# Weighted sums of values in groups of up to three key tiles, in an attention and expert kernel

## What is computed

```
scores = einsum('bhqd,bhkd->bhqk', q, k) * scale        # q, k: 16 content + 32 rotated channels
attn   = softmax(where(causal, scores, -inf))
out    = einsum('bhqk,bhkd->bhqd', attn, v) @ W_o       # v: 16 channels a head
hmid   = gelu(einsum('td,edi->tei', t, W1) + b1)        # 16 experts, 128 hidden channels
eo     = einsum('tei,eio->teo', hmid, W2) + b2          # then the two best experts, weighted
```

## Time and profile before

| what | value |
|---|---|
| median of three runs | 2926.61 us (2926.41 to 2930.67) |
| the profiled execution | 2921.24 us |
| its span | 2919.5 us |
| mean granted TensorE clock | 0.991 |
| TensorE busy | 2809.9 us, 96% |
| VectorE busy | 1863.1 us, 64% |
| ScalarE busy | 1809.6 us, 62% |
| GpSimd busy | 1248.5 us, 43% |

### The profile page before, as it was taken

How to read it: one execution, slowest core, us unless ns; L and a number is a source line. 1 busy time by engine, 2 the same in 40 slices (tenths; PEclk the granted TensorE clock), 3 DMA queues, 4 the chain that set the end, 5 groups by cost and what they waited for, 6 DMA issues and landing times.

```text
span 2919.5 us, 50632 instructions
## 1 busy us (share of the span) xinstructions
PE 2809.9 (96%) x16460; PEld 1236.1 (42%) x16460; DVE 1863.1 (64%) x4636; ACT 1809.6 (62%) x2148; POOL 1248.5 (43%) x1325
## 2 busy tenths in 40 slices
PE   6899999999999999999999999999999999999999
PEld 2344444444444444444444444444444444444433
DVE  4775666756666666666667666675756757667553
ACT  1346675566755677456674576655766566665687
POOL 4312655136451364414654146531465215561254
PEclk8899999999999999999999999999999999999999
DMA  6204443044430444304532055321453124530353
GB/s 146 51 20 99 113 131 78 2 106 120 124 70 4 116 122 109 71 18 118 124 98 64 23 134 127 84 53 43 122 135 88 34 66 120 128 83 25 78 127 94
DMA packets 177551, 253.01 MB, mean 87 GB/s; under 512 B 51085, under 2 KB 83869, under 8 KB 177197
## 3 DMA queue, kind: packets, MB, share of 16 engines
q1 hardware_dynamic: 169936, 246.98, 33.9%
q10 hardware_dynamic: 7360, 2.80, 0.5%
HBM read 159.13 MB, written 12.63 MB: 59 GB/s over the span
## 4 chain that ended last, share of the span: by engine, by line
PE 83%; DVE 7%; issue 4%; POOL 2%; ACT 2%; DMA 1%; SPq 1%; ACTq 0%; POOLq 0%; DVEq 0%
PE ps L1254 17%; PE ps L1296 16%; PE ps L1314 15%; PE ps L1280 9%; PE ps L428 7%; PE ps L477 4%; PE ps L479 2%; PE ps L548 2%; POOL rest L1493 2%; DVE rest L573 1%; PE ps L518 1%; PE ps L529 1%; PE ps L505 1%; PE ps L536 1%; DVE rest L1423 1%
## 5 line engine op out<-in xcount | busy, mean ns | idle before, releaser
L1386 ACT ACTIVATE rest<-ps 128x1024 f32<-128x1024 f32 x1024 | 994.3, 1025 | 340.6 <-PE ps L1296 340.4
L1368 ACT ACTIVATE rest<-ps 128x1024 f32<-128x1024 f32 (+3 forms) x768 | 610.8, 810 | 539.5 <-PE ps L1254 513.7
L1493 POOL TENSOR_TENSOR rest<-rest 128x512 f32<-128x512 f32 x478 | 633.0, 1324 | 560.0 <-DVE rest L1423 549.3
L1423 DVE SCALAR_TENSOR_TENSOR rest<-ps,b2c,wide 128x512 f32<-128x512 f32 x512 | 383.9, 750 | 490.0 <-PE ps L1314 459.2
L1296 PE MATMUL ps<-wide,w1s 98*128 98x512 f32 x2048 | 655.0, 437 | 11.5 <-ACT rest L1386 8.7
L1314 PE MATMUL ps<-rest,w2s 128*32 128x512 f32 x4096 | 546.4, 605 | 0.6 <-ACT rest L1386 0.6
L1483 POOL TENSOR_SCALAR_AFFINE_SELECT rest<-rest 128x256 f32<-128x256 f32 x512 | 207.3, 413 | 770.2 <-ACT rest L1368 768.3
L573 DVE CUSTOM_DVE_ANT_0 rest<-ps,maskd 128x512 f32<-128x512 f32 (+3 forms) x1024 | 444.5, 487 | 111.0 <-PE ps L428 106.3
L1254 PE MATMUL ps<-wide 49*128 49x512 f32 (+3 forms) x2304 | 485.6, 510 | 9.2 <-ACT rest L1368 4.2
L1296 PEld LDWEIGHTS ps<-wide,w1s 98*128 98x128 f32 x2048 | 340.8, 188 | 301.6 <-ACT rest L1386 189.7
L576 DVE TENSOR_REDUCE front<-ps 128x1 f32<-128x512 f32 x512 | 329.1, 685 | 93.2 <-PE ps L428 89.4
(11 more groups left out here) (138 smaller groups left out, 2185.5 us busy)
## 6 DMA issues: line engine op xcount, KB each, us to landing
wide<-gate_rows SPq DMA_DIRECT2D x1024, 128.0 KB, 2.8
wide<-front SPq DMA_DIRECT2D x480, 64.0 KB, 2.0
wide<-front SPq DMA_DIRECT2D x192, 128.0 KB, 2.4
ao<-in_x SPq DMA_DIRECT2D x16, 512.0 KB, 5.0
heads<-front SPq DMA_DIRECT2D x64, 128.0 KB, 2.3
xs<-in_x SPq DMA_DIRECT2D x16, 512.0 KB, 5.1
out<-xs SPq DMA_DIRECT2D x32, 256.0 KB, 2.7
wide<-ao SPq DMA_DIRECT2D x96, 64.0 KB, 2.3
```

The source lines that it names most:

```text
L1368: nc.scalar.activation(L.pt[:, u % PTS, :, f:HALF], L.ps[:, 2 * (u % 2):2 * (u % 2) + 2, 0:HALF - f], ACT.Exp, scale=SCALE).then_inc(S["c_ ...
L1386: nc.scalar.activation(L.hm[:, u % HM, :], bank(2 * (u % 2), 2), ACT.Gelu).then_inc(S["e_gelu"], 1)
L1423: v.scalar_tensor_tensor(out=dst, in0=bank(L2 + q % 2), scalar=L.b2c[:, e:e + 1], in1=L.gb[:, q // 2 % GB, q % 2, :], op0=ALU.add, op1=ALU ...
L1493: g.tensor_tensor(dst, dst, L.gy[:, k % GY, :], ALU.add).then_inc(S["e_add"], 1)
```

## The change

Values are no longer summed after every second slot. `GROUPS` says after which slot which slots' values are summed: in a row of four tiles 2 and 2 as before, in a row of eight 3, 3 and 2. In the long row of slots 8 to 15, the groups stood behind slots 10, 12, 14 and 16, and now stand behind 11, 14 and 16. That is 20 groups an image in place of 24. For this `PTS` grows from 6 to 8, the waits on ScalarE follow, and the SBUF for two more buffers comes from the values: heads lie 17 words apart in place of 32, so that a head's 32 columns of weights run on into the next head's values; the columns behind the 17th go to PSUM rows that nobody reads. 16 zeros close the array.

```diff
+VS = HD + 1
-PTS = 6
+PTS = 8
-FRONT_WORDS = 15248
+FRONT_WORDS = 14176
-REST_WORDS = 10496
+REST_WORDS = 11520
...
-        L.va = self.take("front", NT, NH, VW)
+        L.va = self.take("front", NT, NH, VS)
+        L.va_end = self.take("front", VW // 2)
+        L.va_all = self.view("front", 0, NT * NH * VS + VW // 2)
...
-    g.memset(L.va[:, :, :, HD + 1:VW], 0.0).then_inc(L.S["f_one"], 1)
+    g.memset(L.va_end, 0.0).then_inc(L.S["f_one"], 1)
...
+def value_groups():
+
+    groups, first = {}, 0
+    for g, c in SEQ:
+        for n in ((2, 2), (3, 3, 2))[c]:
+            groups[first + n] = range(first, first + n)
+            first += n
+    return groups
...
-                    mm = pe.matmul(bank(PVB)[h * VW:(h + 1) * VW, f:HALF], L.va[:, j, HG * g + h, :],
+                    mm = pe.matmul(bank(PVB)[h * VW:(h + 1) * VW, f:HALF], L.va_all[:, VS * (NH * j + HG * g + h):VS * (NH * j + HG * g + h) + VW],
...
-                    if s and s % 2 == 0:
-                        values(img, s - 2)
-                        values(img, s - 1)
+                    for N in GROUPS.get(s, ()):
+                        values(img, N)
...
-                if N >= 3:
-
-                    act.wait_ge(S["c_pv"], N - 2)
+                if N >= 4:
+
+                    act.wait_ge(S["c_pv"], N - 3)
+                elif N == 3 and img:
+
+                    act.wait_ge(S["e_add"], 15 * NQ // NE)
...
-                    act.wait_ge(S["c_pv"], NM - 2 + u // 2)
+                    act.wait_ge(S["c_pv"], NM - 3 + u // 2)
```

More of the change, by code:

```diff
@@ L261, in place @@
         L.ot = self.take("rest", 2, HALF)
-        self.begin("rest", REST_WORDS - 2 * HALF)
         L.junk_a = [self.take("rest", HALF) for _ in range(2)]
@@ L908, in __init__ @@
         self.m01 = e.lay.view("rest", 5376, 2 * C)[0:B]
-        self.m25 = e.lay.view("rest", 8448, 4, C)[0:B]
+        self.m25 = e.lay.view("front", FRONT_WORDS - 4 * C, 4, C)[0:B]
         self.g1 = e.lay.view("rest", 0, 2, C)[0:B]
@@ L1196, in sums_done @@
     return SEQ.index((g, c)) if j == 4 * c + 3 else None
+def value_groups():
[5 more added lines that the diff above has]
+    return groups
+GROUPS = value_groups()
 def unit(u):
@@ L1341, in _ @@
                     if q == 0:
-                        values(img, NM - 2)
-                        values(img, NM - 1)
+                        for N in GROUPS[NM]:
+                            values(img, N)
                     if q:
```

## The result

The changed kernel takes 2927.22 us in the median of 22 runs (2923.05 to 2931.71); the kernel before, run beside it, 2922.19 us (22 runs, 2918.56 to 2930.67). The medians differ by 5.0 us; the ratio is 1.0015, 95% interval 1.0010 to 1.0021, so slower by 4.4 us (2.9 to 6.1), inside the 0.2% that the forecast called no change. The profiled execution took 2926.50 us with a span of 2924.7 us, 5.3 us more than before's 2921.24, at the same mean granted clock (0.990 and 0.991). The forecast, 2929.0, lies 1.8 us off, but part of that is luck: it stood on a median of three runs that was 4.4 us above the later one. The difference is the fair measure: +2.4 forecast, +4.4 measured.

What follows compares the result with a forecast made beforehand. TensorE, with work in 96% of the span, was taken as the bound. Rows 0.22 + 0.1 - 0.32 + 0.3 = 0.30 us an image, x 8 = +2.4, gave 2923.6 profiled, 2929.0 us median; 8-in-10 range 2917 to 2937.

Steps and rivals of the forecast that it cites:

- The first row: Slots 9 to 15: one change-over saved, more than given back in two waits for VectorE, +0.22 us an image.
- the second's: Slots 24 to 31: same pattern of pairs as slots 9 to 15, estimated at +0.1 us an image.
- The layout, the ring and the new waits at nothing: 17-word weight spacing, ring of 8 buffers and the new wait for GpSimd's last add: each taken to cost 0.
- Weight loads: Loads at line 1280 should stay at 109 ns; rival: slower at odd addresses, up to +17.4 us, chance 0.04.
- The price of a change-over: On TensorE, each group of values costs about 0.34 us beside its work; 32 fewer would save 10.9 us.
- The walk: Following TensorE's queue through each long row of the third image by durations between starts, giving each row's gain or loss.
- the first rival: Waits for VectorE and ScalarE move but don't grow; whole saving stays: -10.9 us, 2915.7 us, chance 0.22.
- Third row: Slots 32 to 39: the whole saving stays, as slots 36 and 37 have no pair VectorE holds up, -0.32 us.
- Fourth row: Slots 40 to 47: no pairs, scores wait for ScalarE's exponentials; +0.34 us, taken as +0.3 an image.
- First image taken as the others: The first image has other pairs in its slots but was counted like the rest, in 8 x 0.30 us.
- Waits before line 1254 that ScalarE ended should have grown: Sign to check: TensorE's idle time there ended by ScalarE should grow, above all in slots 45 and 46.
- VectorE's reads: Rival: six slots' pairs lose cover and cost a further 0.2 us each, +9.6 us, 2938.6 us, chance 0.15.

Runs made afterwards that it cites:

- the short reads: VectorE reads only the first 64 columns of each pair part, on the changed layout: groups of two 2864.48 us, groups of 3, 3, 2 2861.68 us.
- Half exponentials: From the second image ScalarE takes exponentials of half a unit's queries, on the changed layout: groups of two 2908.28 us, groups of 3, 3, 2 2913.53 us.
- the layout alone: The changed kernel with the old groups of two everywhere, keeping 17-word heads, 8 buffers and new waits: 2923.14 us, ratio 1.0002 to the kernel before.
- the group of four: The changed kernel with groups 2, 3, 3 in slots 32 to 39, 2, 2, 4 in slots 40 to 47, twos elsewhere: 2924.64 us, ratio 1.0011 to before.
- 2, 2, 1, 3: The changed kernel with these group sizes in slots 40 to 47 alone, twos elsewhere: 2913.86 us, ratio 0.9970 to the kernel before.
- the third row alone: The changed kernel with groups of 3, 3, 2 in slots 32 to 39 only, twos elsewhere: 2925.98 us, ratio 1.0013 to the kernel before.
- 2, 3, 3 everywhere: The changed kernel with groups of 2, 3, 3 in place of 3, 3, 2 in all rows of eight: 2925.65 us, ratio 1.0013 to the kernel before.

## Why the prediction was right, and where it was off

*Right.* Near no change because what is saved is given back in waits for VectorE and ScalarE: shown. The first row was forecast within 0.03 us at every start in the lines above, and the short reads show that its loss, and the second's, is VectorE's. Half exponentials show that the last row's is ScalarE's. The direction and the order of rows came out; the row sum did by half only (+0.30 forecast, +0.61 measured), and part of the closeness of the total is the luck named above. The layout, the ring and the new waits at nothing: shown by the layout alone. Weight loads stayed at 109 ns: shown.

*The price of a change-over, 0.34 us, was too high.* It had three parts: 0.14 in and out, 0.10 at the next score's second pass, 0.09 to 0.12 before the group. The second does not belong to the group: with scores in front of it slot 43 has the same 0.54 to its second pass (962.43 to 962.97 with half exponentials). Where four scores stand in a row with no partner late, joining saves the third, 0.10, beside the 0.14. The walk used starts, so this left its row sums nearly alone, but the first rival's full saving would have been 32 x 0.24 = 7.7 us and not 10.9. The Trainium skill (TensorEngine Tiling (Array Packing), Key Properties) says that a change of tiling mode drains TensorE; the runs agree that it costs something and put 0.24 us on it.

*Third row, -0.32, measured -0.14.* The term off is the two 384-wide scores of slot 37, forecast at 0.75 and 0.74; they take 0.81 and 0.85, 0.17 more. Their width was scaled rightly, for before they took 1.49 together. What I put at nothing is ScalarE in this row: without values between slots 36 and 37 the exponential of slot 36 ends at 939.14 and the score that needs its banks starts at 939.19. With half exponentials and threes the two take 1.42.

*Fourth row, +0.3, measured +0.41.* The walk gave +0.34 and I took +0.3; the other 0.07 is slot 43's two units at 1.98 and not 1.91.

*First image taken as the others.* It has +1.05 in slots 33 to 41 where the others have -0.14, because a pair of its own behind slot 35 loses its cover and waits 1.15 us for VectorE; this is the term that the forecast left out. The +0.75 in slots 8 to 17 goes with the granted clock and comes with the layout alone as well. The clock and the opening move a single execution by more than the forecast's whole effect.

*Waits before line 1254 that ScalarE ended should have grown.* They fell, from 69.5 to 58.2 us, while those before line 1295 grew by as much. That longer groups leave fewer first scores behind a group would explain the fall and isn't shown; the growth that I followed at slots 45 and 46 is there but smaller than it. The sum was a badly chosen sign: by the table the effect was in that stretch.

*Rivals.* The saving did not stay whole (the interval excludes a gain). VectorE's reads did not cost 0.2 a place beyond the walk. The rival that I didn't name is the one worth having: the order of group sizes at the end of the attention, where TensorE waited 0.56 behind the last group for the gelu. No row of mine reached past slot 47.

## What to carry to other kernels

Fewer changes between two kinds of matmul are worth their price only where no partner engine used the shorter runs to catch up; follow the queue row by row with starts, as one choice of group size can lose in one row and gain in the next. Put work that is free to move into idle time that is already there (here behind a table load) before counting what merging it saves. Where images repeat, compare a stretch in each of them: 0.2 us an image can be read in rows within 0.02, while totals move by several us with the opening and the granted clock. When a row is off in one image alone, look at the clock of that stretch before the code.

## What was not expected of the hardware

Entering and leaving 128-row, 32-column matmuls between 49-row, 128-column ones cost 0.14 us, and 0.10 more at the score ahead, where no partner is late.

A table load between the last exponential and the first gelu takes 1.28 us, and the gelu starts 0.01 us behind it (970.83 + 1.28 to 972.12 in the trace of the group of four). In the trace of 2, 2, 1, 3 it starts 0.01 us behind the last exponential (973.68 + 0.66 to 974.35). The Trainium skill (ScalarE: Activation LUTs, What ACT_TABLE_LOAD costs) states the same 1.28 us and a drain of 1.38 more for every switch; here such a time stands neither ahead of the load nor between it and the activation, so the measurement decides for 1.28. The load stands behind its activation's wait for the output buffer, for it waited 2.14 us with the gelu behind it; but it does not stand behind the input, for in the other trace it ran from 974.35 while the inner matmuls that the gelu reads, issued from 974.20, were still in work.

The opening differs from execution to execution. Slot 0 of the first image comes between 4.2 us earlier and 1.9 later than before in kernels that have the change's opening and differ from it only further on, and slots 0 to 8 then take up to 4.7 us more, with a granted clock of 0.67 between 70 and 100 us and 0.88 to 0.90 in the 20 us behind, where the others have 0.72 or more and 1.00.

The granted clock also falls to its lower level further on, at places that differ between the traces: the third row alone has 0.51 from 227.6 to 231.0 us, in a group of values that takes 4.38 us for 2.71, and 2, 3, 3 everywhere has 0.50 in images 2 and 3 where before has 1.00. What brings it about isn't shown.
